# An order change in a sequence layer with routed experts on one Trainium2 core

## The reference

```python
y   = einsum(states, C).real + x @ D_mat.T          # states: scan over time of B x
x   = layernorm(x + (x + sigmoid(res_logit) * (gelu(y @ W1) @ W2)))
weights, indices = top_k(softmax(x @ Wg), 2)        # 2 of 8 experts a token
for e in range(8):
    h = gelu_exact(x @ FW1[e] + fb1[e])             # 128 -> 512
    out += (h @ FW2[e] + fb2[e]) * weight_of(e)     # 512 -> 128
x   = layernorm(x + out)
```

## Time and profile before

| What | us |
|---|---|
| runs | 326.46, 327.86, 327.94 |
| median of the runs | 327.86 |
| the profiled execution | 325.67 |
| its span, first to last instruction | 323.9 |

### The profile page before, as it was taken

How to read it: one execution, slowest core, us unless ns; L and a number is a source line. 1 busy time by engine, 2 the same in 40 slices (tenths; PEclk the granted TensorE clock), 3 DMA queues, 4 the chain that set the end, 5 groups by cost and what they waited for, 6 DMA issues and landing times.

```text
span 323.9 us, 5155 instructions
## 1 busy us (share of the span) xinstructions
PE 277.0 (86%) x1265; PEld 210.0 (65%) x1265; DVE 253.3 (78%) x758; ACT 217.3 (67%) x482; POOL 220.7 (68%) x269
## 2 busy tenths in 40 slices
PE   0789799989999968598499999999999999999720
PEld 0524365545554525576299999999999999984200
DVE  1766725896796768999969999999999999985660
ACT  1716547554374460667459999999999999991590
POOL 3634663506878875787777787777777878876870
PEclk9999959999999997789969999999999999999985
DMA  2731353210110112215432323323323322851382
GB/s 63 244 97 35 106 151 102 65 32 16 49 44 33 57 41 56 79 46 196 147 102 74 97 66 102 92 79 97 98 69 98 98 76 90 299 206 33 89 260 65
DMA packets 27188, 31.17 MB, mean 96 GB/s; under 512 B 4632, under 2 KB 22560, under 8 KB 27160
## 3 DMA queue, kind: packets, MB, share of 16 engines
q1 hardware_dynamic: 22328, 20.89, 21.8%
q0 software_dynamic: 4832, 9.97, 9.2%
HBM read 16.99 MB, written 13.86 MB: 95 GB/s over the span
## 4 chain that ended last, share of the span: by engine, by line
PE 60%; DVE 13%; POOL 9%; DMA 6%; issue 6%; ACT 3%; SPq 1%; DVEq 0%; ACTq 0%; POOLq 0%
PE bank L1079 12%; PE bank L1081 12%; PE bank L1080 12%; PE bank L1120 5%; POOL slots_d L476 5%; PE bank L1169 3%; PE bank L1193 3%; PE bank L1142 2%; PE bank L1110 2%; PE bank L1087 2%; PE bank L1096 2%; DMA late<-in_L_ffn_W_dram 2%; PE bank L1111 2%; PE bank L1108 1%; ACT h L558 1%
## 5 line engine op out<-in xcount | busy, mean ns | idle before, releaser
L482 POOL DMA_INDIRECT results_d<-work,dest x87 | 97.4, 1120 | 26.4 <-issue 25.2
L476 POOL DMA_INDIRECT slots_d<-rows,slot_i x64 | 68.4, 1069 | 19.9 <-issue 19.9
L620 ACT ACTIVATE h<-bank,buse 128x384 f32<-128x384 f32 x116 | 67.8, 585 | 11.3 <-PE bank L1081 8.3
L977 DVE TENSOR_TENSOR h_l<-h,h_h 128x384 fp32r<-128x384 f32 x116 | 64.7, 558 | 6.0 <-ACT h_h L625 4.0
L1079 PE MATMUL bank<-h_h,wuse 128*128 128x384 f32 (+1 forms) x132 | 54.9, 416 | 1.9 <-DVE h_l L977 1.7
L1079 PE MATMUL bank<-xt_h,wuse 128*128 128x384 f32 x116 | 41.5, 357 | 6.7 <-DVE xt_l L963 3.0
L1080 PE MATMUL bank<-h_l,wuse 128*128 128x384 f32 (+1 forms) x132 | 46.2, 350 | 0.0
L1081 PE MATMUL bank<-h_h,wuse 128*128 128x384 f32 (+1 forms) x132 | 45.8, 347 | 0.0
L940 DVE CAST wuse<-fw 128x1024 fp32r x58 | 40.4, 697 | 1.7 <-issue 1.7
L1081 PE MATMUL bank<-xt_h,wuse 128*128 128x384 f32 x116 | 40.8, 352 | 0.0
L1080 PE MATMUL bank<-xt_l,wuse 128*128 128x384 f32 x116 | 40.7, 351 | 0.0
(11 more groups left out here) (216 smaller groups left out, 535.9 us busy)
## 6 DMA issues: line engine op xcount, KB each, us to landing
late<-slots_d SPq DMA_DIRECT2D x29, 195.0 KB
late<-in_L_ffn_W_dram SPq DMA_DIRECT2D x16, 256.0 KB, 2.7
work<-in_L_attn_x3d_dram SPq DMA_DIRECT2D x8, 256.0 KB, 3.2
rows<-results_d SPq DMA_DIRECT2D x4, 512.0 KB, 5.4
work<-results_d SPq DMA_DIRECT2D x4, 512.0 KB, 7.0
slots_d<-zeros SPq DMA_DIRECT2D x9, 195.0 KB, 2.4
results_d<-work,dest POOLq DMA_INDIRECT x87, 2.5
slots_d<-rows,slot_i POOLq DMA_INDIRECT x64, 2.4
```

The costliest lines, as they stand in the source:

```text
L476: pool.indirect_dma_start(out=slots_d, out_offset=bass.IndirectOffsetOnAxis(ap=slot_i[:, k, i:i + 1], axis=0), in_=rows[:, k, i, :], in_of ...
L482: pool.indirect_dma_start(out=results_d, out_offset=bass.IndirectOffsetOnAxis(ap=dest[:, SQ * g + q:SQ * g + q + 1], axis=0), in_=yo[:, g ...
L620: act.activation(h32[:, b % 2, 0:SLOTS], H_PS[b % 2][:, 0:SLOTS], ACT.Gelu, bias=buse[:, k, b:b + 1]).then_inc(sm["gelu_b"], 1)
L977: dve.tensor_tensor(ht_l[b], h32[:, b % 2, 0:SLOTS], ht_h[b].bitcast(F32), ALU.subtract).then_inc(sm["hbl_ready"], 1)
```

## The change

**Weights.** There are three staging slots in place of two, and the pieces are dealt differently (3, 6 and 7 to the set-up and chunks 0 and 1). On ACT a chunk's four GELUs now come first, then the copy of x of the chunk after next, rows_of of the chunk before the last (it was the last), up to three casts, y of the next chunk, and the other casts. On PE the transposes of the rows of the chunk before stand behind y of the next chunk. On POOL two subtractions stand ahead of the norm (three before), the others behind it.

**Routing in the chunks.** On DVE the choice comes ahead of the statistics, the slots behind the first splits, turn_back behind the residual. In chunk 7 the tables of tiles 0 to 2 follow the ranks at once, and the first tile's weights stand ahead of the residual; the exponents of group 2 move behind the residual of chunk 6. On POOL the first four dispatches of a group's first half stand ahead of the norm.

**Behind the chunks.** On DVE the first split of tile 0 comes directly behind the last logits; the tables of tiles 3 to 8 follow it. The last statistics move to the cut ahead of tile 1, the last ranks to the cut ahead of tile 2, the last weights into `resume`, ahead of the last tables. ACT follows: rows_of of chunk 6 behind the first high part, of chunk 7 at the cut ahead of tile 2, the last tanh into `resume`.

**End.** SP loads the last tile's rows ahead of the results. PE's first final sum is made inside the last tile's steps, and the sum banks are taken in another order. The final norms of POOL run over two chunks at once for chunks 1 to 4.

The diff, without the renaming of the staging slots and of the semaphores that follows from their number, and without the body of the paired norm, which does the old operations on a longer range:

```diff
 SPLIT = 2
-PIECES = (0, 3, 8, 13, 16)
+PIECES = (0, 3, 9, 16)
+STAGES = 3
 YO = 20
...
-                wait(sp, sm["fw_lo"], n - 1)
-                sp.dma_start(fw_stage_in(n), fw_src(n)).then_inc(fst_loaded[n % 2], 16)
+                if n == STAGES - 1:
+                    sp.wait_ge(sm["setup_sb"], 1)
+                    sp.wait_ge(sm["cs_ready"], 1)
+                wait(sp, sm["fw_lo"], n + 1 - STAGES)
+                sp.dma_start(fw_stage_in(n), fw_src(n)).then_inc(fst_loaded[n % STAGES], 16)
-            for n in range(2):
+            for n in range(STAGES - 1):
                 weights(n)
...
             ready = GC * (NG - 1)
+            load(MT - 1, (MT - 1) % 2)
             for i in range(3):
...
             sp.wait_ge(returned[3], 16 * SQ * (DONE - kept))
-            for c in range(2):
-                results(c)
-            load(MT - 1, (MT - 1) % 2)
-            for c in range(2, ready):
+            for c in range(ready):
                 results(c)
...
                 fw_now = list(pieces(c + 1))
-                for n in fw_now[:3]:
+                for n in fw_now[:2]:
                     weights_low(n)
+                group, half = (c - GC - 1) // GC, (c - GC - 1) % GC
+                done = 2 if half == 0 else QT + 2 if c == NCH else QT
+                if c >= GC + 1:
+                    dispatch(group, QT * half, done)
                 if c >= 1:
                     norm(c - 1)
-                for n in fw_now[3:]:
+                for n in fw_now[2:]:
                     weights_low(n)
                 if c >= GC + 1:
-                    half = (c - GC - 1) % GC
-                    dispatch((c - GC - 1) // GC, QT * half, QT * (half + 1))
+                    dispatch(group, done, QT * (half + 1))
             dispatch(NG - 1, 0, GT)
...
                 send_back(g)
-            final_norm(0)
+            final_norm(0, 1)
             send_back(MT - 1)
-            for c in range(1, NCH):
-                final_norm(c)
+            for a, b in ((1, 3), (3, 5), (5, 6), (6, 7), (7, 8)):
+                final_norm(a, b)
...
                         act.activation(h_fp[:, b - SPLIT, :], H_PS[b % 2][:], ACT.Gelu_apprx_tanh).then_inc(sm["h_act"], 1)
-                    if b == 1 and c + 2 < NCH:
-                        x_copy(c + 2)
-                    for n in fw_now[b:b + 1]:
-                        weights_high(n)
+                if c + 2 < NCH:
+                    x_copy(c + 2)
+                if c >= 2:
+                    rows_of(c - 2)
+                for n in fw_now[:3]:
+                    weights_high(n)
                 if c + 1 < NCH:
                     y_copy(c + 1)
-                for n in fw_now[HB:]:
+                for n in fw_now[3:]:
                     weights_high(n)
-                if c >= 1:
-                    rows_of(c - 1)
                 if c in CHOOSING:
...
             x_high(0, 0)
+            rows_of(NCH - 2)
...
+                softmax_tanh(NG - 1)
                 x_high(FRESH, FRESH % 2)
...
             walk(MT, FRESH, step, resume,
-                                {1: lambda: rows_of(NCH - 1),
-                                 2: lambda: softmax_tanh(NG - 1),
+                                {1: lambda: act.wait_ge(sm["rt_ready"], NCH),
+                                 2: lambda: rows_of(NCH - 1),
                                  **{YO + 1 + GROUP * i: sent_back(i) for i in range(3)}})
...
                 chosen = CHOOSING.get(c)
+                last = c == NCH - 1
                 if g is not None:
                     route_ranks(g)
-                    route_slots(g)
+                if last:
+                    route_tiles(0)
                 hidden_low(c, 0)
...
                 if g is not None:
+                    route_slots(g)
                     route_weights(g)
...
                     logits(c - 1)
-                    stats(c - 1)
-                    aggregate(c - 1)
                 if chosen is not None:
...
                     route_choice(chosen, 1)
+                if c >= 1:
+                    stats(c - 1)
+                    aggregate(c - 1)
+                if chosen is not None:
                     route_hits(chosen)
+                if last:
+                    first_weights()
                 if c + 2 < NCH:
                     turn_in(c + 2)
-                    turn_back(c + 2)
-                if chosen is not None:
-                    route_exponents(chosen)
+                    if chosen is not None:
+                        route_exponents(chosen)
...
                                          op0=ALU.mult, op1=ALU.add).then_inc(sm["r_ready"], 1)
+                if c + 2 < NCH:
+                    turn_back(c + 2)
+                elif chosen is not None:
+                    route_exponents(chosen)
...
+            def first_weights():
+                dve.wait_ge(sm["fw_lo"], NFW)
+                dve.wait_ge(sm["route_ready"], 1)
+                held.extend(expert_of(g) for g in range(2))
+                weights1(0, 0, held[0])
+                weights2(0, 0, held[0])
             for c in range(NCH):
                 chunk(c)
-                if c >= NCH - 2:
-                    route_tiles(c + 2 - NCH)
-                if c == NCH - 2:
-                    dve.wait_ge(sm["fw_lo"], NFW)
-                    dve.wait_ge(sm["route_ready"], 1)
-                    held.extend(expert_of(g) for g in range(2))
-                    weights1(0, 0, held[0])
-                    weights2(0, 0, held[0])
             logits(NCH - 1)
-            stats(NCH - 1)
-            aggregate(NCH - 1)
             x_low(0, 0)
...
             meta(0, 0)
+            route_tiles(1)
             route_choice(NG - 1, 0)
...
+            def last_stats():
+                stats(NCH - 1)
+                aggregate(NCH - 1)
             def last_ranks():
...
+                route_weights(NG - 1)
                 route_last_tiles()
...
-            walk(MT, FRESH, step, resume, {1: last_ranks, 2: lambda: route_weights(NG - 1)})
+            walk(MT, FRESH, step, resume, {1: last_stats, 2: last_ranks})
...
                     logits(c - 1)
-                    r_transposed(c - 1)
...
                     outputs(c + 1)
+                if c >= 1:
+                    r_transposed(c - 1)
                 wait(pe, sm["r_ready"], c)
...
+            def x1_sum(c):
+                wait(pe, sm["f_r"], c + 1 - len(SUM_PS))
+            def result_sum(c):
+                pe.wait_ge(y_loaded[c], 16)
...
                     hidden(g, k, 3)
+                if prev and not now and g == MT:
+                    result_sum(0)
                 if prev:
...
                             xt(g + 2, k)
+                        if b == HB - 1 and g == MT - 1:
+                            x1_sum(0)
                         pe.wait_ge(sm["hbl_ready"], HB * g + (b + 1))
...
             logits(NCH - 1)
-            r_transposed(NCH - 1)
             xt(0, 0)
...
             xt(1, 1)
+            r_transposed(NCH - 1)
...
-            x1_before = {0: [0], 1: [1], 2: [2], 3: [3, 4, 5], 4: [6, 7]}
-            for c in range(NCH):
+            x1_before = {1: [1], 2: [2], 3: [3, 4, 5], 4: [6, 7]}
+            for c in range(1, NCH):
                 for n in x1_before.get(c, []):
+                result_sum(c)
```

53 lines of the change are left out of this document (27 added, 26 removed).

## The result

The changed kernel takes 337.67 us (median of four runs) against 327.9 of the kernel before run beside it: 1.033 times as long, 95% interval 1.028 to 1.039. Forecast were 330.7 and a range of 325.5 to 333.5. The direction was right, the size was not: the profiled execution has a span of 334.8 us against 323.9, so 10.9 us came where 2.8 were summed up.

What follows compares the result with a forecast made beforehand. TensorE bounds the attention chunks, VectorE chunk 7 to tile 3, TensorE the tile loop, then a short chain. Tile 3 +3.8 and tail -1.0 give +2.8 on 325.67: 328.5, or 330.7 on the median's scale; range 325.5 to 333.5.

Steps and rivals of the forecast that it cites:

- Part 1: Weight casts, chunks 1 and 2: a 9.3 us chain makes PE wait 3.0 us in chunk 2; chunk 3 starts +0.4.
- Part 2: Routing, chunks 3 to 6: norm of chunk 5 starts at 112.0, so VectorE's chunk 7 begins at most 0.5 us earlier.
- Part 3: Chunk 7 to the last residual: up to 1.7 us of VectorE's 1.69 us idle go; last residual moves -1.2.
- Part 4: Behind the chunks: two new VectorE gaps, +2.4 and +2.6; fills and row load hidden by 1 to 2 us.
- first gap: VectorE between the last residual and tile 0's split, with only the logits copy ahead of it: 2.4 us lost.
- second gap: VectorE ahead of the last weights, which wait for the tanh behind tile 2's last scaling: 2.6 us lost.
- The sum for tile 3: Shift of tile 3's split on VectorE: -1.2 + 2.4 + 2.6 = +3.8 us, ends +1 and +7.
- Part 5: GpSimd's last dispatches and first send-back: +7.5 us, made up at 0.7 a tile; at most 1 us left at the end.
- GpSimd becomes the bound: Rival, chance 0.08: last sixteen dispatches 2.5 us later than forecast, tile 9's load late, TensorE stands; 334 at 3 us over.
- Part 6: Tail: first final sum inside the last tile gives -1.0 us; paired norms and the earlier last row load give nothing.
- attention gains in full: Rival, chance 0.17: no 3.0 us wait or cold stretch in chunk 2, chunk 3 near 59.2; total -3, 324.8 us.

Runs made afterwards that it cites:

- e3: Changed kernel with GpSimd's norm ahead of all dispatches of its step again; 333.8 to 342.2 us, ratio 1.013 to the kernel before.
- e4: Changed kernel with the last tables ahead of the last weights in VectorE's list; 339.87 us, ratio 1.030 to the kernel before.
- e12: Changed kernel without the send-backs of tiles 1 and 4 (six transfers less on GpSimd); 333.11 us, ratio 1.021 to the kernel before.
- e8: Kernel before with four GpSimd operations, 4.2 us in all, added ahead of the first send-back; 332.8 us, ratio 1.017.
- e5: Changed kernel with the end as before (late last row load, first sum behind the last tile, single norms); median 345.68 us, 338.3 to 349.2.
- e2: Changed kernel with pieces dealt 3, 6, 4 and 3, so casts 13 to 15 follow chunk 2's GELUs; 329.9 and 331.8 us, ratio 1.011.
- e17: The fast version run again, beside the kernel with only the part behind the chunks as before; 322.36 us, ratio 0.984 to the kernel before.
- e10: Changed kernel with the tables of tiles 3 to 8 again ahead of the last logits on VectorE; 338.56 us, ratio 1.040 to the kernel before.
- e13: Kernel before without the send-backs of tiles 1 and 4 (six transfers less on GpSimd); 327.42 us, ratio 1.002.
- The fast version: Changed kernel with casts dealt 3, 6, 4 and 3 and everything behind the chunks as before; 321.92 and 322.36 us in two runs.
- e6: First run of the fast version (casts dealt 3, 6, 4 and 3, behind the chunks as before); 321.92 us, ratio 0.987 to the kernel before.

## Why the prediction was wrong

**Part 1, right in mechanism, short in size.** The chain from the transposes of chunk 0 to chunk 2's first GELU was there, and it was 10.5 us long, not 9.3: the wait is 4.43 us in place of 3.0. What was longer shows in GpSimd's subtractions and, under them, in VectorE's scan, first that beside them and then one of chunk 5:

```profile
48.01 1.27 POOL L458 TENSOR_TENSOR fw<-late,fw 128x512 fp32r<-128x512 f32 x1
```
```profile
49.23 2.18 POOL L458 TENSOR_TENSOR fw<-late,fw 128x512 fp32r<-128x512 f32 x1
```
```profile
48.05 2.30 DVE L735 TENSOR_TENSOR_SCAN work<-rdec,work 128x512 f32<-128x512 f32 x1
```
```profile
102.32 1.23 DVE L735 TENSOR_TENSOR_SCAN work<-rdec,work 128x512 f32<-128x512 f32 x1
```

The first subtraction took 1.27 us, the second 2.18; the scan, which began beside the first and ended beside the second, took 2.30, not 1.23. The rule of the Trainium skill, SBUF — State Buffer, section "Who interferes with whom", that operations of VectorE with two inputs in SBUF and operations of GpSimd that read SBUF exclude each other, was given up to 1.4 us in the prediction and left out of the sum. The trace agrees, with 0.91 us on that subtraction; the load (from the subtraction's end at 51.41 to the cast at 54.42, 3.0 us against 2.7) and the hand-overs took the rest of the 1.4 us by which the wait is longer. The chance of an operation in that place should have been counted: VectorE's list had a scan there.

**Part 2, wrong step.** "Whatever else chunks 3 to 6 gain ends in that wait" for the norm of chunk 5. Two waits came nearer to TensorE, each by way of ACT's list:

```profile
110.40 1.51 ACT L541 ACTIVATE rows<-bank,nmr,rstd 128x128 f32<-128x128 f32 x4 [2.67 <-POOL nmr L469]
...
117.16 0.26 ACT L591 ACTIVATE early<-early 128x72 f32<-128x72 f32 x1 [4.11 <-DVE early L840]
```

The norm of chunk 4 now stands behind four dispatches too, ACT's rows of chunk 4 behind the norm, and TensorE's next transposes behind the rows (1.41 us). When dispatches were moved ahead of the norm, I followed the norm to the exponents and not to rows_of and the transposes' bank. The second wait (1.30 us) has another chain, and e3 still has it (1.29): the exponents of group 2 come at 116.81 (before 113.96), behind the residual of chunk 6, done at 116.52, and the norm of chunk 5 that I had followed, done at 116.70. But they also let ACT's tanh go, only at 117.16, and the GELUs of chunk 7 and the rows of chunk 5 stand behind it. That chain is read from the rows; no run takes it apart. e3 shows that the first wait is exchanged for others, since the list is full. And the norm of chunk 5 came 3.4 us behind its forecast of 112.0: 1.3 with the first dispatch, and 2.1 because the 24 dispatches and three norms ahead of it took 39.8 us and not 37.7.

**Part 3, wrong.** The idle of 1.69 us did not go; it is 1.36 us at its new place, just ahead of the last residual (the expert number is still read just ahead of its use):

```profile
128.04 1.36 DVE L961 CAST wuse<-fw 128x1024 fp32r x2 [1.36 <-issue]
```

And VectorE's part of chunk 7 began later, with a residual of chunk 6 at 115.77 (before 114.49) and the exponents behind it. So +0.9 in place of -1.2.

**Part 4, right, and the sum too small for the first gap.** The second gap is 2.56 us (forecast 2.6). The first is 3.1 (2.4), 0.8 more came in two small waits. That the fills and the row load lie just under the split was right as a bound: they held TensorE 6.21 us and VectorE 0.37, and e4 shows that they would have held it for 2.42 had the second gap gone. The sum for tile 3 was 3.7 short: 2.1 from the residual, 0.7 from the first gap, 0.8 from the small ones.

**Part 5, the step that failed.** GpSimd began 10.5 us late, not 7.5, and "at the end I expect at most 1 us" did not come: it sends the last tile back 9.9 us late. The step took the 0.7 us a tile by which GpSimd is shorter than TensorE for cover. It was none already in the kernel before: from 176.20 to 296.00 its 84 send-backs stand 0.30 us behind one another (26.4 us idle for 87 in the earlier trace rows), so the list had no wait into which a later start could go, save the 1.98 us ahead of the norm. What GpSimd gains on TensorE only shortened its distance to the tile that it sends, from 14.9 us after the last scaling of tile 3 to 1.45 after that of tile 27, 0.56 a tile. In the changed kernel the distance goes from 17.6 to 5.8. So +10.5 at the start, +1.3 for longer send-backs, less the wait: +9.9. Carried through like this, the forecast's own +7.5 would have given +5.5 at that place. The rival "GpSimd becomes the bound", at a chance of 0.08, was what happened, though not by the load of tile 9: behind tile 3 TensorE waits for no load.

Along the tiles, the 8.1 us that the sum lacks are 3.7 at tile 3's start, 0.4 in the loop, 2.0 by which GpSimd ends later than the loop, and 2.0 behind the last send-back (+1.0 in place of -1.0; why stays open). So a GpSimd on time would not have saved the whole: the norm of the first sums stood 3.8 us behind its statistics, and e12 won 4.1 to 4.6.

**Part 6.** The first sum's -1.0 could not show, and "nothing, since nobody waits for that load now" was wrong for a late GpSimd: 4.26 us in e8, 12.72 in e5. The earlier load kept the changed kernel from losing more.

**The rival "attention gains in full"** did not happen, but e2 and e17 show that it was one number away: with the casts dealt otherwise the chunks gain what that rival said (chunk 3 at 59.76, it said 59.2).

## What to carry to other kernels

Before an in-order list gets a later start, look at the waits that it has up to its end: a list without a wait in it has no cover, however much it gains a tile. When a step is moved behind others, follow every reader of its result one engine further than the first, and price the operations of a neighbour that stretch it. Work that hides a wait is not moved without other work put in its place.

## What the hardware showed unexpectedly

The send-backs' mean duration is not a constant: 1107 to 1200 ns (e8, e3) in traces of nearly the same list, 8 us over 84. In these traces the span ends 20.6 to 22.6 us behind the last send-back (before 303.3 and 323.9, changed 313.2 and 334.8, e10 316.1 and 337.7, e13 303.3 and 325.9), so this scatter is a scatter of the whole.

What makes it differ shows in the timelines, here of the changed kernel:

```profile
223.03 1.68 POOL L484 DMA_INDIRECT results_d<-work,dest  x1 [0.30 <-issue]
```
```profile
223.91 0.68 DVE L961 CAST wuse<-fw 128x1024 fp32r x1
```

In each of the 20 traces the send-backs of 1.5 us and more begin 0.83 to 0.89 us ahead of one of VectorE's casts of a tile's weights and end 0.11 to 0.13 us behind its end; send-backs with no such cast beside them mostly take 0.96. Before has 3 of these long ones, the changed kernel 7 and 5, e10 14, e3 and e12 16. The fast version was profiled twice (e6, e17): tile 3's split is at 156.39 and 156.11, the long ones are 5 and 13, the mean is 1135 and 1180 ns, and the spans are 318.0 and 322.1 us. So the time of one and the same kernel hangs on how GpSimd's list stands to VectorE's. That the cast holds the send-back is read from these ends and not tested, since no run moves the casts; what sets how the two lists meet in an execution stays open.
